# Weight sums from DRAM instead of GpSimd, and the first product accumulated in the second one's bank, in a Strassen feed-forward of a decoder layer

## The reference

```python
x = layernorm(x + attention(x, Wq, Wk, Wv, Wo))          # 16 heads, scores*mask/sqrt(512)
x = layernorm(x + expert_ffn(x, tokens, ctx, ctx, ctx))  # token id picks 1 of 4 experts, 512x512 each
h = silu(x @ w_gate) * (x @ w_up)                        # 512 -> 2048
h = keep_2_largest_of_every_4(h)
x = layernorm(x + h @ w_down)                            # 2048 -> 512
```

## Time and profile before

| | us |
|---|---|
| median of 3 runs | 1158.88 (1153.5 to 1162.85) |
| the profiled execution | 1152.48 |
| its span, first to last instruction | 1150.7 |
| attention, until | some 420 |
| expert stage | 420 to 560 |
| rounds 0 to 15, first product of round 0 to last of round 15 | 549.8 to 1089.9 |
| down products of the last four d, norms, output | to 1150.7 |

### The profile page before, as it was taken

One profiled execution on the slowest core, in us unless ns is written; L12 is line 12 of the kernel. 1 busy time (PEld: TensorE's weight loads), 2 busy tenths in 40 slices (PEclk: granted clock), 3 DMA queues, 4 the chain that ended last, 5 costly groups with the idle time before them and its releaser, 6 DMA issues.

```text
span 1150.7 us, 18114 instructions
## 1 busy us (share of the span) xinstructions
PE 1023.0 (89%) x5830; PEld 817.5 (71%) x5831; DVE 888.2 (77%) x1889; ACT 605.0 (53%) x1141; POOL 536.5 (47%) x640
## 2 busy tenths in 40 slices
PE   7989999998999769999986998889959989899886
PEld 6667777776777648788775876767747767678665
DVE  5898799688778865665759486675988889777894
ACT  5787588578758952234364323453543423544424
POOL 2194457347445613223457355563443557445224
...
GB/s 265 247 203 183 85 194 219 102 180 175 193 59 175 212 109 65 75 121 135 101 74 37 38 73 37 8 67 37 74 3 34 74 37 91 51 14 101 18 20 73
DMA packets 61081, 116.78 MB, mean 101 GB/s; under 512 B 6976, under 2 KB 9024, under 8 KB 60992
## 3 DMA queue, kind: packets, MB, share of 16 engines
q1 hardware_dynamic: 56112, 101.48, 32.2%
...
## 4 chain that ended last, share of the span: by engine, by line
PE 34%; DVE 13%; ACT 5%; DMA 5%; issue 4%; POOL 2%; SPq 1%; POOLq 0%; DVEq 0%; ACTq 0%
PE f_bank L53 20%; PE f_bank L1955 12%; DVE h_lo L2356 4%; DMA w_raw<-gate 3%; ACT h_hi L2120 2%; DMA wd_raw<-down 2%; DVE beats L2323 2%; ACT w_hi L2047 1%; DVE h L2347 1%; PE f_bank L1829 1%; ACT wd_hi L2055 1%; DVE h L2299 1%; ACT h L2102 1%; PE f_bank L1837 1%; DVE x_lo_T L2267 1%
## 5 line engine op out<-in xcount | busy, mean ns | idle before, releaser
L53 PE MATMUL f_bank<-wd_hi,h_hi 128*128 128x512 f32 x256 | 109.0, 426 | 48.8 <-DVE h_lo L2356 43.4
L714 ACT ACTIVATE probs<-bank,nmax 128x384 f32<-128x384 f32 (+3 forms) x256 | 131.7, 549 | 21.4 <-DVE nmax L899 19.2
L883 DVE CUSTOM_DVE_ANT_0 bank<-bank,mask 128x384 f32<-128x384 f32 (+3 forms) x256 | 123.0, 502 | 13.7 <-PE bank L510 12.8
L521 PE MATMUL bank<-ident,probs 128*128 128x128 f32 x640 | 108.7, 284 | 24.5 <-DVE pt_lo L908 11.1
L908 DVE TENSOR_TENSOR pt_lo<-bank,pt_hi 128x512 f16<-128x512 f32 (+1 forms) x192 | 114.8, 598 | 16.7 <-ACT pt_hi L724 16.3
L2097 ACT ACTIVATE h<-f_bank 128x512 f32<-128x512 f32 x64 | 37.4, 596 | 165.1 <-PE f_bank L1955 163.7
L724 ACT ACTIVATE pt_hi<-bank 128x512 f16<-128x512 f32 (+1 forms) x192 | 104.9, 546 | 23.4 <-PE bank L521 22.9
L1740 POOL TENSOR_TENSOR w_lo<-w_raw,w_hi 128x512 fp32r<-128x512 f32 x48 | 82.7, 1738 | 63.4 <-ACT w_hi L2047 63.3
L1955 PE MATMUL f_bank<-x_hi_T,w_hi 128*128 128x512 f32 x256 | 101.4, 396 | 6.7 <-ACT h L2097 2.7
L53 PE MATMUL f_bank<-wd_lo,h_hi 128*128 128x512 f32 x256 | 106.5, 416 | 0.0
L53 PE MATMUL bank<-x_hi,w_qk 128*128 128x512 f32 x256 | 100.7, 412 | 6.2 <-DVE x_lo L913 5.7
...
## 6 DMA issues: line engine op xcount, KB each, us to landing
...
```

Of the source, the lines that this page charges most:

```text
L53: ins = pe.matmul(out, a(k, i), b(k, j), start=(n == 0), stop=(n == len(chain) - 1))
L521: ins = pe.transpose(TP[u % TR][:, j * P:(j + 1) * P], probs[u % RP][:, j * P:(j + 1) * P], ident[:, :])
L714: ins = act.activation(probs[u % RP][:, at:at + cols(r)], S[u % SR][:, at:at + cols(r)], ACT.Exp, bias=nmax[:, r, c:c + 1])
L883: dve.tensor_tensor_reduce(out=S[u % SR][:, at:at + cols(r)], in0=S[u % SR][:, at:at + cols(r)], in1=mask[:, T - cols(r):T], scale=1.0, sc ...
```

## The change

- **Sums in DRAM.** The host lays gate and up out by halves. A DRAM tensor `sums_dram` (4 x 8 x 128 x 512) holds the four sums for all 8 units of 256 hidden columns. In the expert stage SP copies up[0], up[0], gate[0], gate[1] into it, 2.1 MB each, DRAM to DRAM, ahead of the row loads of tile 3 and on. GpSimd then issues 16 DMAs with `accum_op=ADD`, 512 KB each, that add up[1], gate[0] and two of the sums: two after tile 0 (behind a wait for all four copies), one after tile 2, one after tile 4, three each after tiles 6, 7, 9 and 12, each batch behind a wait for the earlier ones that it reads. `weight_sums` is gone.
- **Weights product by product.** SP loads each of the 7 sources (256 KB for a and b) into a place of its own in `w_raw` once that product's b half of the round before is done. ScalarE and VectorE or GpSimd cut them in the order 1, 6, 5, 7, 2, 4, 3; GpSimd has 6, 7, 4 and VectorE 1, 5, 2, 3.
- **P1 into P2's bank.** `copy(L, "1a"/"1b")` writes FB instead of SBUF, P2 is accumulated on it (`start` false), Silu reads FB; the adds "11a", "11b" are gone. 2a waits for the copy of 1a, the copy of 1b for Silu of a, 2b for the copy of 1b. Signs of three token blocks and of the weights are turned, and Silu has scale -1.
- **Order.** VectorE: in even rounds `early` has the whole chain of d = L-1, then (every round but 8) `kept_lo(L-2)` and weight "1", ahead of "22a". ScalarE: Silu of a behind the magnitudes, copy 1b behind it; `kept_hi(L-2)` ahead of copies 7a, 7b. `mag_of` is d % 3.

```diff
+            for n, of in enumerate((up[0], up[0], gate[0], gate[1])):
+                sp.dma_start(sums_dram[n].rearrange("u p n -> (u p) n"),
+                             of.rearrange("u p n -> (u p) n")).then_inc(s_draw, 16)
             tiles(sp, step)
             block_in(2)
-            weights_in(1)
...
+            def sum_weights(at, of, units, waits):
+
+                wait_apart(pool, s_passed, waits)
+                for u in units:
+                    pool.dma_start(sums_dram[at, u:u + 2].rearrange("u p n -> (u p) n"),
+                                   of[u:u + 2].rearrange("u p n -> (u p) n"), accum_op=ALU.add,
+                                   max_dma_last_dim=8192).then_inc(s_order, 16)
+
+            FIRST, OTHERS = (0,), (2, 4, 6)
+            sums_at = {0: ((0, up[1], FIRST, [(s_draw, COPIED)]), (1, gate[0], FIRST, [(s_draw, COPIED)])),
+                       2: ((2, sums_dram[0], FIRST, [(s_order, 32)]),),
+                       4: ((3, sums_dram[2], FIRST, [(s_order, 48)]),),
+                       6: ((0, up[1], OTHERS, [(s_order, SUMMED[0])]),),
+                       7: ((1, gate[0], OTHERS, [(s_order, SUMMED[0])]),),
+                       9: ((2, sums_dram[0], OTHERS, [(s_order, SUMMED[0] + 96)]),),
+                       12: ((3, sums_dram[2], OTHERS, [(s_order, SUMMED[0] + 144)]),)}
...
             for n in range(NS):
                 ln2.rstd(pool, n, n % 4, False)
                 place(n)
-                if n == 2:
-                    weight_sums(0)
...
+                for sum_of in sums_at.get(n, ()):
+                    sum_weights(*sum_of)
...
+            def weight_in(L, X):
+                n = weight(L, X)
+                if X in "5673":
+
+                    sp.wait_ge(s_order, SUMMED[L > 1])
...
+                    sp.wait_ge(s_pr, product_done(L - 1, X + "b"))
+                sp.dma_start(both(raw, X), weight_source(L, X)).then_inc(s_wraw[n % RW], 16)
```

and VectorE's round:

```diff
             def early(L):
 
-                if L == LB + 1:
-                    compare(L - 2)
-                    count_first(L - 2)
-                    count_second(L - 2)
-                    choose(L - 2)
-                elif L >= 2 and L % 2 == 0:
-                    compare(L - 1)
+                if L >= 2 and L % 2 == 0:
+                    chain = L - 1 if L != LB + 1 else L - 2
+                    compare(chain)
+                    count_first(chain)
+                    count_second(chain)
+                    choose(chain)
+                if L >= 2 and L != LB + 1:
+                    kept_lo(L - 2)
...
                 early(L)
+                if more:
+                    weight_lo(L + 1, "1")
                 add_product(L, "22a")
                 add_product(L, "22b")
                 if more:
-                    weight_lo(L + 1, 0)
-                add_product(L, "11b")
+                    weight_lo(L + 1, "5")
                 gated_first(L, 0)
-                if more:
-                    weight_lo(L + 1, 2)
                 gated_first(L, 1)
-                if L >= 2:
+                if L == LB + 1:
                     kept_lo(L - 2)
                 add_product(L, "12a")
                 add_product(L, "12b")
```

ScalarE's copies and Silu:

```diff
+                if name == "1b":
+
+                    act.wait_ge(s_silu, NS + 4 * L + 1)
+                elif name == "1a" and L > 0:
+
+                    act.wait_ge(s_silu, NS + 4 * (L - 1) + 2)
+                to = FB[:, :] if name[0] == "1" else {"6": us, "7": hv[hslot[L, 1]]}[name[0]][:, i, :]
+                act.activation(to, VB[i][:, :], ACT.Copy).then_inc(s_cp, 1)
...
+                if r == 0:
+                    act.wait_ge(s_pr, product_done(L, "2" + "ab"[i]))
...
+                    x, of = hv[hslot[L, 0]][:, i, :], FB[:, :]
+                else:
+                    act.wait_ge(s_ad, added(L, "12" + "ab"[i]))
+                    x = of = us[:, i, :]
+                act.activation(x, of, ACT.Silu, scale=-1.0).then_inc(s_silu, 1)
```

More of the change, by code:

```diff
@@ L1486, in late @@
             free_slots = [hslot[2 * (d // 2) + half, d % 2] for half in range(2)] + free_slots
-    assert all(hslot[L, r] < 6 for L in range(ROUNDS - 1) for r in range(2))
     with ExitStack() as ctx:
@@ L1607, in late @@
         NTURN = 2 * RW
-        first_group = {12 + g: g for g in range(GROUPS)}
+        first_weight = {12 + i: X for i, X in enumerate(FREED)}
+        MADE = ROUNDS
+        COPIED = 16 * 4
+        SUMMED = (16 * 4, 16 * 16)
         def chunk(L):
@@ L1784, in round_ @@
             def round_(L):
-                if L + 1 < ROUNDS:
-                    weight_sums(L + 1)
                 if L >= 2 and L % 2 == 0:
                     down_lo((L - 2) // 2)
-                if L + 1 < ROUNDS:
-                    for g in range(1, GROUPS, 2):
-                        weight_lo(L + 1, g)
+                if L + 1 < MADE:
+                    for X in FREED:
+                        if X in LO_ON_POOL:
+                            weight_lo(L + 1, X)
                 if L == 2:
@@ L2135, in round_ @@
                 s, odd = divmod(L, 2)
-                more = L + 1 < ROUNDS
-                soon = L >= 3 and odd and more
+                more = L + 1 < MADE
                 copy(L, "1a")
-                copy(L, "1b")
-                if L == 0:
-                    token_hi(0, "T4")
-                    token_hi(0, "B22")
                 if L == LB + 1:
@@ L2168, in round_ @@
                     magnitudes(s - 1, 1, 1)
-                for g in range(2 if soon else 0, 4) if more else ():
-                    weight_hi(L + 1, g)
-                silu(L, 0, 1)
-                for g in (4, 5) if more else ():
-                    weight_hi(L + 1, g)
                 if L == LB:
@@ L2181, in round_ @@
                 silu(L, 1, 1)
-                if more:
-                    weight_hi(L + 1, 6)
+                for X in ("7", "2", "4") if more else ():
+                    weight_hi(L + 1, X)
                 if L == LB:
@@ L2467, in round_ @@
                 add_product(L, "12b")
-                if more:
-                    weight_lo(L + 1, 4)
                 gated_second(L, 0)
```

295 lines of the change are left out of this document (142 added, 153 removed).

## The result

The changed kernel takes 1167.46 us (median of 10 runs, 1160.58 to 1168.78); the kernel before, over its 10 runs, 1158.32. The ratio is 1.0076, with a 95% interval of 1.0052 to 1.0100: slower by 0.8%. The prediction said 1144, faster. The profiled executions differ by more than the medians (spans 1165.1 and 1150.7), since that of before took 1152.48, less than any of its 10 runs. What follows compares spans, 14.4 us apart, where the medians are 9.1 apart; in which stage the 5 us between the two lie, no run shows.

A forecast was written before the change was run, and what follows sets the result against it. TensorE's queue was taken to pace the FFN, with gaps from `h_lo` waits and VectorE's chain as second limit. FFN -40 and expert stage +25 gave -15: 1144 us from the median 1158.9, forecast range 1130 to 1154, whole range 1116 to 1176.

The forecast's parts named there:

- the 3 us for the adding DMAs: Expert stage: GpSimd's issue of adding DMAs and its wait at tile 9 cost 3 in all (0 to 20).
- the 40 us to be saved in the FFN: FFN rounds: savings of 18.5 odd, 15 even, 4 round 8, 2 rounds 0 to 2, 1 rounds 14 and 15; bounds 15 and 55.
- copies: Expert stage: 8.4 MB of DRAM copies end at 457 and stall TensorE 18 us (7 to 28), plus 2 of clock.
- odd rounds 3, 5, 13: FFN: these rounds fall to 30.0 us with no wait on `h_lo`, each saving 3.7.
- odd rounds 9, 11: FFN: round 11 saves the 3.8 us over 30.0, round 9 less; taken as 3.7 each.
- the prediction's other case: Expert stage: if rows came past the copies, the stall would be 12.6 us, by GpSimd's wait.
- 3a waits 1 to 2.2 us: Even rounds: product 3a waits this long for "22a" on VectorE; 2.5 taken, with 1.4 of clock, giving 33.9 us a round.
- The earliest use is '1': Every round: weight loads are hidden; weight "1" is wanted 6 us after issue, later landing pushes `kept_hi` and the P7 copies.
- 2a must now wait for a copy behind the token conversions: Round 0: 2a waits some 5 us, paid back by Silu and gated products no longer waiting for weight sums.
- The wait only changes place: Rival, 8%: even rounds stay at 37.5 as "22a" is late instead of `h_lo`; 25 saved, 25 lost, 1159 us.
- The slower rival: Rival, 22%: in the expert stage copies stall 28 + 2 and adds 23 at tile 9; 53 less 40, 1172 us.
- the signs that the prediction listed as proof against itself: Gap at 439 over 30 us, adding-DMA waits at several tiles, or waits on P1 or P7 copies or weight loads every round.

The follow-up runs named there:

- e2: Changed kernel with the four DRAM copies and GpSimd's wait for them, but no adding DMAs, sums left as plain copies: 1152.16 us, 0.9937 of before.
- e1: Changed kernel without the DRAM copies and adding DMAs, sums not made, plain gate and up blocks read instead: 1137.31 us, 0.9818 of before.
- e12: Changed kernel with second chain moved, scatters moved, round 0's P1a copy earlier, DRAM sums spread; against that, `kept_lo` put back behind `gated_first`: 1119.78 us, 0.9647 of before.
- e5: Kernel before, in its own order, without GpSimd's weight sums, up and gate loaded a second time in their place: 1151.92 us, 0.9901 of before.
- e8: Changed kernel with the even rounds' whole chain (not round 8's) moved from ahead of `kept_lo` and "22a" to between the down adds: 1146.03 us, 0.9844 of before.
- e11: Changed kernel with second chain moved, scatters moved, P1a copy earlier, DRAM sums spread; against that, "22a", "22b" ahead of finished rows' work: 1090.54 us, 0.9407 of before.
- e9: Changed kernel with second chain moved; against that, token-number scatters only after rounds 2 and 4, round 0's P1a copy ahead of T3's conversion: 1129.58 us, 0.9717 of before.

## Why the prediction was wrong, by its own steps

Two terms failed: the 3 us for the adding DMAs, which cost 14.7, and the 40 us to be saved in the FFN, of which 14.6 came.

| step | predicted | measured | by |
|---|---|---|---|
| copies | +20 (stall 18, clock 2) | +13.3 | e2 less e1 |
| adding DMAs | +3 | +14.7 | after less e2 |
| odd rounds 3, 5, 13 | -11.1 | -12.2 | table of rounds |
| odd rounds 9, 11 | -7.4 | +1.5 | same |
| even rounds 10, 12 | -7.4 | -3.9 | same |
| even rounds 4, 6 | -7.5 | +0.7 | same |
| round 8 | -4 | -8.3 | same |
| rounds 0 to 2 | -2 | +7.2 | same |
| rounds 14, 15 | -1 | +1.8 | same |
| round 7, tail | 0 | -0.6 | same |
| issue costs, rounding | +2 | +0.1 | e1 less before, start of round 0 |

**Right.** `kept_lo` ahead of "22a" was a gain: rounds 3, 5 and 13 are 29.9 long (round 3 at a granted clock of 1.00), forecast 30.0, and e12 gives the waits back when only that is undone. But it gives back 1.5 of the 4.0 us that round 13 gained: the wait is 1.1 with 0.3 of clock there, and was 2.0 with 1.9 before. What took the other 2.5 off, the adds "11a" and "11b" gone from VectorE, or `kept_hi` early on ScalarE, was not separated; the GpSimd sums did not, by e5. A gap costs its length and up to 1.9 of clock, as read before (1.6 in e12). The copies hold the rows, in one gap; its 12.4 us come near the 12.6 of the prediction's other case, rows that pass the copies, by chance only, since TensorE's wait ended on the rows. Silu from PSUM and the sign in its scale cost nothing that a steady round shows: 29.9 is what TensorE's queue alone needs.

**The expert stage came out near, 28.1 for 25, by luck: two errors cancel.** The copies land by 452.8, not 457, and the gap is 12.4, not 18:

```profile
452.77 0.95 POOL L1757 DMA_DIRECT2D sums_dram<-up  x1 [9.85 <-DMA sums_dram<-gate]
```

From the first issue at 422.85 the 8.39 MB took 29.9 us or less, 280 GB/s, so the mean over the queue, which gives 31 us, was the better guess than the 33 taken: 4 us of the miss. The other 1.6 is that TensorE ran dry at 440.7, not 439.0. The Trainium skill (DMA: Bandwidth & Descriptors, "Latency and other measured facts") has 207 to 214 GB/s per direction, for copies in tiles of 128 rows of 16 KiB at a well chosen pitch; the measurement decides against it for these four long contiguous copies. The adding DMAs were the step that failed here. "I take 3 in all" priced only GpSimd's wait at tile 9. The cost lies elsewhere, in other transfers of the same engines: rows, `rows_kept`, first weights. Of the 14.7, 8.8 are waits on such transfers and 4.8 the lower clock behind them. Its upper bound, 20, held it, by another cause.

**The FFN failed: 40 less forecast, with bounds of 15 and 55, 14.6 less measured.** Four terms were missed.
1. Even rounds, "3a waits 1 to 2.2 us": it waits 4.2 in round 10. The walk was right up to `choose` (+13.9 for +13.4), but `kept_lo` took 4.54, beyond its bound of 3.9, and weight "1" 1.74 for 0.6, beside `down_lo`. In round 2 the wait is 12.4. Five sums of `wins` beside `down_lo`, 1.5 to 1.7 each for 0.4 to 0.7, are some 5 of it; most of the rest is that the first chain begins 4.1 us into the round (635.13), where that of round 10 begins 6.3 ahead of it (914.99), since round 1 has no down product and lasts only 20.7. Round 2 had not been walked at all, and round 14 was given the wait of the others, 2.5, and has 4.2. e8 shows the cause by removing it.
2. "The earliest use is '1', issued at +2.9 and wanted by ScalarE at +9": the sentence named its own risk, a landing over 6 us. It took 14 in round 4. The walk named no row of a load beside the scatters, which the change doesn't touch. "A round early" is true of the product that uses weight "1", but ScalarE cuts it in the round in which it is asked for.
3. Round 11 was taken to gain 3.8 as the model of odd rounds. But in 9 and 11 the statistics and norms of finished rows stand ahead of "22a". This is in the code of `early`, and e11 shows its price: round 11 falls from 34.7 to 29.9, round 9 from 37.9 to 32.0.
4. Round 0, "2a must now wait for a copy behind the token conversions (some 5 us), paid back": the wait is 7.6 and it is not paid back, 2.8 longer. e9 takes it away by one line (26.7).

**The rivals.** "The wait only changes place" had 8% and was nearest to what the even rounds 4, 6, 10 and 12 do: 36.6 in the mean, for its 37.5 and the forecast's 33.9. The slower rival named 1172 near the truth but by another cause: it put 53 us into the expert stage, and there were 28. By its own reckoning the sign turns only above 40 us of stalls; it turned below that, since the FFN gave a third of its forecast. Of the signs that the prediction listed as proof against itself, two are in the trace: late transfers beside adding DMAs at several tiles, and waits on weight loads, though in rounds 4 and 6 alone; a wait on the copy of P1, 7.6 us, is there in round 0.

**Left open.** Whether it is the order of the queue or the bandwidth by which the copies hold the rows of tile 3 was not separated; nor why e1's rounds 11 and 12 differ by 1.2 and 2.2 from those after. A kernel without the scatters was not tried. Open too are the 5 us by which the spans lie further apart than the medians, and the 9 us of e5 that its trace doesn't show. In e11 rounds 2, 7 and 8 remain above 34 us.
